# Moving the first two products of an FFN into the Mamba passes ahead of it

## The chip, the cores and the metric

The kernel runs on one core of one Trainium2 chip. The metric is the device time of one execution in microseconds, lower is better. The time before is 3401.91 us, the median of 3 runs (3400.91 to 3403.28).

## The reference, cut to what matters

The input x is (4, 2048, 256), float32. A Mamba layer is computed, then a feed-forward network (FFN) with ternary weights and a scale for each output column, each followed by a residual and a layer norm:

```python
xz = einsum('bld,ed->ble', x, in_proj_w); xs, z = xz[..., :512], xz[..., 512:]
u = silu(conv4(xs) + conv_b)                      # depthwise, 4 taps
dt_lo, B, C = split(einsum('bld,ed->ble', u, x_proj_w), (64, 16, 16))
delta = softplus(einsum('blr,dr->bld', dt_lo, dt_proj_w) + dt_proj_b)
h = exp(delta * A) * h + (delta * u) * B          # a scan over 2048 positions
y = (sum over n of h * C + u * D) * silu(z)
x1 = layernorm(x + einsum('bld,ed->ble', y, out_proj_w))
g = silu(x1 @ w1.T * s1) * (x1 @ w2.T * s2)       # w1, w2: 1024 x 256
g = gelu(g @ h1.T * sh1); g = gelu(g @ h2.T * sh2)    # h1, h2: 1024 x 1024
out = layernorm(x1 + g @ w3.T * s3)               # w3: 256 x 1024
```

## The kernel before, in words

The work is cut into 16 tiles of 512 positions (`NT`), four to a row of the batch. There are two stages, one after the other: all 16 tiles go through Mamba (`mamba_stage`), x1 is written to HBM, and then all 16 go through the FFN.

**The Mamba stage.** The scan has 64 groups of a tile (`NG`): each is one 128x512 scan on VectorE (`scan`, L759), whose decays ScalarE writes into one of three PSUM banks (`decay_of`, L563), two groups ahead (`EXP_LEAD`). Four groups make a chunk: before it VectorE (three chunks of four, L743) or GpSimd (the fourth, L645) makes the input `db`, behind it GpSimd multiplies with C (`times_c`, L634) and TensorE sums over n (`fold_step`, L412); behind every fourth chunk VectorE adds u*D (`skip`, L783). Each engine runs the same list by hand: `tile(t)` goes through slots i = 0 to 63, and in slot i it handles group i + 20 (`OFF`), so that from slot 44 on it scans the next tile. Beside the scan the slots hold everything else, one tile ahead: convolutions in slots 0 to 15 (L350, copies L485), silu of u in slot 17 (L494), the x_proj product in 18 to 21 (L364), z in 26 to 33 (L337, copies L482), silu of z in slot 40 (L490), spread rows (L391, copies L512) in 42 to 54, the products of the tile after (L325, copies L555) in 47 to 53, softplus in several (for the second quarter in slots 39 to 43: L521 to L536 on ScalarE, L766 and L770 on VectorE), the output product in 55 to 60 (L430). The layer norm of the tile before is in slots 1 to 11: statistics on VectorE, a few small steps on GpSimd in slot 8, and in slot 11 ScalarE writes x1 into `res` (L582). All queues are in order, and an instruction waits for semaphores; so a slot's place in a queue is also what it delays. All DMAs are issued by SyncE (SP): rows of delta to HBM (L248, L250), broadcasts back (L256, L265), inputs, x1.

**Between the stages** `round_weights` loads all FFN weights in 20 pieces of 128x1024 and 8 of 128x256, rounds them to float32r on ScalarE (L1236), and VectorE and TensorE check that the rounding lost nothing; the result is a flag (L1253), and all engines branch on it: with ternary weights the branch for exact weights (`split`) is taken.

**The FFN stage** (`ffn_stage`, split). Every activation is held as two float32r parts (high: a ScalarE copy, L1059; low: the difference, VectorE, L1123), so a product takes two matmuls. A tile on TensorE is: `hidden` layer 0, `hidden` layer 1 (128 matmuls of 512 columns each, L961, with the 8 transposes of the next x1, L973, in layer 1), `output` (64 matmuls of 256 columns, L1020), then `gated` of the next tile (64 matmuls of 512 columns on x1, L961 with `s_x_t`). ScalarE applies Silu in `gated` (L1066) and Gelu in `hidden` (L1082). The PSUM banks are two each for w1, w2, hidden and output.

In PSUM during the Mamba stage banks 0 and 1 are `p_mm`, 2 is `p_dt`, 3 `p_b`, 4 `p_y`, 5 to 7 the decays.

Of the kernel before, what the change touches and what calls it, by code (L numbers as in the profile page):

```python
# [5 lines left out]
F32 = mybir.dt.float32  # L6
# [77 lines left out]

OFF = 20
CONV_SLOTS = range(0, KI * TAPS)
SILU_U_SLOT = 17
# [16 lines left out]
EXP_LEAD = 2  # L104

# [25 lines left out]
def mamba_stage(nc, sems, xT, x, in_wT, conv_w, conv_b, xp_wT, dt_wT, dt_b, A_log, D_param, out_wT,  # L131
                fold, spread, ident, d_rows, du_rows, x1):
    ctx = ExitStack()
    with ctx:
# [23 lines left out]
        x_nat = sb("x_nat", [P, SUB, DM])  # L158
        res = sb("res", [P, SUB, DM])
        xb = sb("xb", [P, KI, TAPS - 1 + NT])  # L160
        uz = [sb(f"uz{i}", [P, 2 * KI, NT]) for i in range(2)]
# [16 lines left out]
        bc = [sb(f"bc{i}", [P, NT], F32R) for i in range(2)]  # L178

# [34 lines left out]
        DECAY0, SCANNED0, SAVED0, HC0, FOLDED0, DVE0, POOL0, OUT0 = 2 * GC, 2 * JC, NK, TURNS * QN, HCSTEPS, 2 * QV, 2, SUB + 1  # L214

        COPIES = 16 * GN

        block = ctx.enter_context(nc.Block())

        WEIGHTS = 12  # L220

        @block.sync
        def _(sp):
# [52 lines left out]
            load_xT(OPENING)  # L276
            copies(OPENING, 0)
# [30 lines left out]
        def _(pe):  # L308
# [21 lines left out]
            def z_product(t, j, k):  # L330
                if k == 0:
                    if j >= 2:
                        pe.wait_ge(z_sb, t.count(KI, j - 1))
                    elif j == 1:
                        pe.wait_ge(xd_sb, t.count(2, 2))
                        pe.wait_ge(xd_lo, t.count(1, 1))
                last = pe.matmul(p_mm[(1 + j) % 2][:], w_in[:, k, DI + j * P:DI + (j + 1) * P], xT_sb[:, k, :],  # L337
# [4 lines left out]
            def conv_product(t, j, k):  # L342
# [7 lines left out]
                last = pe.matmul(p_mm[j % 2][:], w_conv[:, j, k, :], xb[:, j, k:k + NT],  # L350
# [4 lines left out]
            def front(t, i):  # L355
                par = t.tt % 2
                if i in CONV_SLOTS:
                    conv_product(t, *divmod(i - CONV_SLOTS.start, TAPS))
                if i in XD_SLOTS:
# [4 lines left out]
                    last = pe.matmul(p_mm[0][0:DTR + 2 * NS, :], w_xp[:, k, :], uz[par][:, k, :],  # L364
# [8 lines left out]
            def step_sizes(t, c):  # L373
                pe.wait_ge(xd_sb, t.count(2, 2))
                if not (is_first(t) and c == 0):
                    pe.wait_ge(sp_dve, t.count(2 * KI, 2 * c))
                pe.matmul(p_dt[:], w_dt[:, c * P:(c + 1) * P], xd[:], start=True, stop=True).then_inc(dt_mm, 1)

            def rows(t, r):
                nxt = t.following()  # L380
                if r < 2:
                    pe.wait_ge(xd_lo, t.count(1, 1))
                    pe.wait_ge(z_sb, t.count(KI, 3 + r))
                else:
# [31 lines left out]
            def project(t, s, k_first, k_last):  # L416
                pe.wait_ge(gated, t.count(KI, k_last + 1))
# [942 lines left out]
```

## Time and profile before

| | |
|---|---|
| median of 3 runs | 3401.91 us |
| the profiled execution | 3402.25 us, its span 3400.4 us |
| Mamba stage | 0 to about 2021 us of the span |
| weights rounded and checked | about 2021 to 2058 us |
| FFN stage | about 2058 to 3400 us |
| DMA traffic | 223.8 MB in the queue of the kernel's own DMAs |

Busy shares of the whole span are averages over stages of different kinds; the slices of the span show them apart. The granted clock is TensorE's, 1.00 being full.

### The profile page before, as it was taken

To read this page: it belongs to the slowest core of one execution; us is meant where nothing else is said; L and a number is where in the kernel's file an instruction comes from. 1 tells how busy PE (TensorE), PEld (TensorE's weight loads), DVE (VectorE), ACT (ScalarE), POOL (GpSimd) and SP (SyncE) were. 2 spreads that over 40 slices of the span, in tenths; PEclk is the share of its full clock that TensorE was granted. 3 is DMA by queue.
4 is the path that set the end of the run, shared out by engine and by line. 5 is a ranking of instruction groups with operands and counts; after the bars stand their busy time and mean duration, and the time that the engine had idled before them with its cause. 6 is when DMAs were issued, how large, how long until landed. Compare 5 with 4: busy or idle time off the path is not lost. (4 is left out here: it accounts for less than half of the span.)

```text
span 3400.4 us, 37160 instructions
## 1 busy us (share of the span) xinstructions
PE 2667.5 (78%) x10431; PEld 1546.2 (45%) x10432; DVE 2371.5 (70%) x2860; ACT 1817.9 (53%) x2980; POOL 1738.6 (51%) x892
## 2 busy tenths in 40 slices
PE   5666776676676667667667438999999999999997
PEld 2121222122122212212222115888888888888886
DVE  2999999899999999999999964333343344344443
ACT  3667566666666666666675534444444444444442
POOL 1899998898898899898899950000000000000000
PEclk8777877788787788878778657999999999999999
DMA  3344433444433444433444321000000000000000
GB/s 85 85 99 112 107 97 89 106 106 100 111 91 91 106 112 106 97 98 91 99 112 105 96 99 68 13 13 13 13 13 13 12 13 12 13 12 13 12 13 13
DMA packets 138273, 225.80 MB, mean 66 GB/s; under 512 B 14432, under 2 KB 49120, under 8 KB 138080
## 3 DMA queue, kind: packets, MB, share of 16 engines
q1 hardware_dynamic: 138080, 223.80, 26.8%
q14 instruction: 142, 1.16, 0.1%
q8 instruction: 51, 0.84, 0.1%
HBM read 173.42 MB, written 50.33 MB: 66 GB/s over the span
## 5 line engine op out<-in xcount | busy, mean ns | idle before, releaser
L759 DVE TENSOR_TENSOR_SCAN h<-bank,state,db 128x512 f32<-128x512 f32 x1024 | 1250.4, 1263 | 54.9 <-ACT bank L563 28.4
L634 POOL TENSOR_TENSOR hc<-h,c_rows 128x1024 f32<-128x1024 f32 x512 | 1194.9, 2362 | 44.9 <-PE bank L412 34.3
L563 ACT ACTIVATE bank<-d_bc,a_neg 128x512 f32<-128x512 f32 x1024 | 699.2, 687 | 578.8 <-DVE h L759 577.0
L961 PE MATMUL s_bank<-s_act,weights_r 128*128 128x512 f32 x4096 | 935.0, 390 | 0.0
L961 PEld LDWEIGHTS s_bank<-s_act,weights_r 128*128 128x128 f32 x4096 | 768.1, 188 | 158.3
L1123 DVE TENSOR_TENSOR s_act<-s_h,s_act 128x512 fp32r<-128x512 f32 x384 | 262.7, 689 | 638.7 <-ACT s_act L1059 627.0
L391 PE MATMUL bank<-bc,w_spread 64*128 64x512 f32 x272 | 157.7, 604 | 420.9 <-DVE db L743 416.9
L1082 ACT ACTIVATE s_h<-s_bank,s_sc 128x512 f32<-128x512 f32 x256 | 176.0, 688 | 528.8 <-PE s_bank L961 528.6
L743 DVE TENSOR_TENSOR db<-bank,du_bc 128x2048 f32<-128x2048 f32 x192 | 434.7, 2264 | 21.2 <-DMA du_bc<-du_rows 21.1
L412 PE MATMUL bank<-hc,fold_w 128*32 128x512 f32 x2048 | 363.2, 790 | 95.2 <-DVE uz L783 78.7
L645 POOL TENSOR_TENSOR db<-du_bc,b_row 128x2048 f32<-128x2048 f32 x64 | 289.7, 4526 | 118.7 <-DVE h L759 106.2
L391 PEld LDWEIGHTS bank<-bc,w_spread 64*128 64x128 f32 x272 | 59.6, 233 | 632.4 <-DVE db L743 545.7
L350 PE MATMUL bank<-xb,w_conv 128*128 128x512 f32 x512 | 291.8, 700 | 6.5 <-issue 2.6
L1059 ACT ACTIVATE s_act<-s_h 128x512 fp32r<-128x512 f32 x384 | 241.7, 629 | 18.0 <-DVE s_h L1133 9.9
L961 PE MATMUL s_bank<-s_x_t,weights_r 128*128 128x512 f32 x1024 | 237.5, 393 | 1.4 <-DVE s_x_t L1117 1.4
L961 PEld LDWEIGHTS s_bank<-s_x_t,weights_r 128*128 128x128 f32 x1024 | 193.0, 190 | 41.3 <-DVE s_x_t L1117 1.8
L412 PEld LDWEIGHTS bank<-hc,fold_w 128*32 128x32 f32 x2048 | 45.2, 122 | 308.1 <-issue 202.1
L1066 ACT ACTIVATE s_silu<-s_bank,s_sc 128x512 f32<-128x512 f32 x128 | 88.3, 690 | 179.7 <-PE s_bank L961 171.8
L350 PEld LDWEIGHTS bank<-xb,w_conv 128*128 128x128 f32 x512 | 99.2, 214 | 171.9 <-issue 166.9
L364 PE MATMUL bank<-uz,w_xp 128*96 128x512 f32 x128 | 89.4, 814 | 97.4 <-ACT uz L494 97.4
L325 PE MATMUL bank<-xT_sb,w_in 128*128 128x512 f32 x256 | 144.3, 704 | 21.7 <-DVE a_neg L729 15.6
L1133 DVE SCALAR_TENSOR_TENSOR s_h<-s_bank,s_sc,s_silu 128x512 f32<-128x512 f32 x128 | 96.2, 751 | 82.6 <-PE s_bank L961 82.6
(91 smaller groups left out, 2299.0 us busy)
## 6 DMA issues: line engine op xcount, KB each, us to landing
d_bc<-d_rows SPq DMA_DIRECT2D x256, 256.0 KB, 4.7
du_bc<-du_rows SPq DMA_DIRECT2D x256, 256.0 KB, 7.6
d_rows<-sp_r SPq DMA_DIRECT2D x64, 256.0 KB, 2.0
du_rows<-sp_w SPq DMA_DIRECT2D x64, 256.0 KB, 2.0
xT_sb<-in_xT SPq DMA_DIRECT2D x16, 512.0 KB, 9.1
x_nat<-in_x SPq DMA_DIRECT2D x16, 512.0 KB, 4.6
x<-res SPq DMA_DIRECT2D x16, 512.0 KB, 3.2
s_x_nat<-x SPq DMA_DIRECT2D x16, 512.0 KB, 4.4
```

The lines of the kernel that those rows point to most:

```text
L350: last = pe.matmul(p_mm[j % 2][:], w_conv[:, j, k, :], xb[:, j, k:k + NT], start=k == 0, stop=k == TAPS - 1)
L391: pe.matmul(dst[:], spread_w[:, which, :], bc[t.tt % 2][DTR:P, :], start=True, stop=True).then_inc(done, 1)
L412: last = pe.matmul(p_y[GD * j:GD * j + GD, :], fold_w[:], hc[:, k % HCSTEPS, j, :], start=q == 0, stop=q == QN - 1, tile_position=(0, GD * j))
L563: act.activation(decays[DECAY_BANK[g]][:], d_bc[c % 2][:, j, :], ACT.Exp, scale=a_neg[:, g:g + 1]).then_inc(decay, 1)
L634: pool.tensor_tensor(hc[:, k % HCSTEPS, at:at + HG], h[:, H_SLOT[k], at:at + HG], c_rows[:, q, :].unsqueeze(1).broadcast_to([P, HG, NT]), ...
L645: pool.tensor_tensor(db[:, k % DBSTEPS], du_bc[c % 2][:], b_row[:].unsqueeze(1).broadcast_to([P, JC, NT]), ALU.mult).then_inc(db_pool, 1)
L743: dve.tensor_tensor(db[:, k % DBSTEPS], p_b[:].unsqueeze(1).broadcast_to([P, JC, NT]), du_bc[c % 2][:], ALU.mult).then_inc(db_dve, 1)
L759: dve.tensor_tensor_scan(h[:, H_SLOT[k], j, :], decays[DECAY_BANK[g]][:], db[:, k % DBSTEPS, j, :], state[:, g:g + 1], ALU.mult, ALU.add). ...
L961: last = pe.matmul(dst, weights[:, w_at + k * rows_w + cols:w_at + k * rows_w + cols + P], ins[j][:, k, :], start=k == 0 and j == 0, stop= ...
L1059: act.activation(acts[(c // KH) % 2][0][:, c % KH, :], hring[c % 3][:], ACT.Copy).then_inc(hi, 1)
L1082: act.activation(dst, p_h[m % 2][:], ACT.Gelu, scale=sc[:, 2 + layer, m:m + 1]).then_inc(gelu, 1)
L1123: dve.tensor_tensor(a[1][:, c % KH, :], hring[c % 3][:], a[0][:, c % KH, :].bitcast(F32), ALU.subtract).then_inc(lo, 1)
```

## The change

The products of x1 with w1 and w2 are made in the Mamba stage, one tile behind the norm, and go through HBM (`ab`, 16 x 256 KB for each tile). New in each `tile(t)` of the Mamba stage, where t is the tile whose residual is formed and x1 is that of the tile before it:

- TensorE: `ffn(t, i)` is called first in each slot. Slots 13 and 17: transposes of `res` (k = 0, 1; 4 blocks each, plain float32 matmuls against the identity). Slots 15 and 19: the same 4 blocks again and one float32r matmul that takes the high part off. Slots of `AB_PLACES`: 16 products of 4 float32r matmuls of 512 columns, into banks 0 to 2.
- ScalarE: last in slots 14, 16, 18, 20 a copy of `x_t`; last in the slot after each product a copy of it to one of three buffers; first in the slot after that its store, a DMA that ScalarE issues; behind every second copy a load of 256 KB of w1 and w2.
- SP: the load of x goes straight into `res` (the buffer `x_nat` is gone), behind `copies(t, 3)`, and waits for the store of x1 and the transposes.
- u of quarter 0 is in one buffer `u0` for both tiles: the convolutions run in the order 1, 2, 3, 0, and the Silu of u is two instructions.
- At the start w1 and w2 (2 MB) are loaded into buffers of h, rounded on ScalarE in slots 2 and 8 of the pass before the first tile, and stored to HBM in pieces of 256 KB; VectorE waits for the roundings before its first tile. After the last tile the transposes and 16 products of the last x1 run by themselves (`PAST`).
- `round_weights` still checks all 28 pieces, but keeps only h1, h2, w3.

In the FFN stage (`split_stage`) `transposes` and the products of `gated` are gone. SP loads pairs of products into a ring of four; ScalarE applies Silu to four at a time in SBUF (slot m = 1 of each layer), then one high copy at m = 2 to 5; VectorE follows with product and low part. `hidden` has four PSUM banks in place of two.

```diff
+CONV_ORDER = (1, 2, 3, 0)
+XT_PLACES = ((13, 2), (17, 1))
+AB_PLACES = ((25, 0), (30, 2), (32, 2), (34, 2), (35, 1), (36, 2), (38, 1), (40, 1), (41, 0), (44, 2), (46, 2),
+             (48, 2), (50, 2), (52, 2), (60, 2), (62, 2))
+ABRING = 3
...
 # SP, tile(t)
-                sp.wait_ge(out_sb, t.count(SUB, OUT0))
+                copies(t, 3)
+                sp.wait_ge(x1_out, t.count(16, 16))
+                sp.wait_ge(xt_mm, t.count(KM, KM))
-                sp.dma_start(x_nat[:], x[t.b, rows, :].rearrange("(s p) c -> p s c", p=P)).then_inc(x_in, 16)
-                copies(t, 3)
+                sp.dma_start(res[:], x[t.b, rows, :].rearrange("(s p) c -> p s c", p=P)).then_inc(x_in, 16)
...
 # TensorE
+            def transpose(dst, k, alone):
+                for s in range(SUB):
+                    last = pe.matmul(dst[:, s * P:(s + 1) * P], res[:, s, k * P:(k + 1) * P], w_id[:].bitcast(F32),
+                                     start=s == 0, stop=alone and s == SUB - 1)
+                return last
+            def transposed(t, k, step):
+                dst = bank[XT_PLACES[k][1]]
+                if step == 0:
+                    if k == 0:
+                        pe.wait_ge(ln_out, t.count(SUB, SUB))
...
+                    elif exists(t.following()):
+                        pe.wait_ge(conv_sb, t.following().count(KI, KI))
+                    transpose(dst, k, True).then_inc(tr_mm, 1)
+                elif step == 2:
+                    pe.wait_ge(xt_hi, t.count(KM, k + 1))
+                    transpose(dst, k, False)
+                    pe.matmul(dst[:], w_id[:], x_t[0][:, k, :], start=False, stop=True).then_inc(xt_mm, 1)
+            def ffn_product(t, e):
+                m, which = divmod(e, 2)
...
+                for k in range(KM):
+                    for j in range(2):
+                        last = pe.matmul(product_bank(t, e)[:], w12_sb[m % 2][:, which, k, :], x_t[j][:, k, :],
+                                         start=k == 0 and j == 0, stop=k == KM - 1 and j == 1)
+                last.then_inc(ab_mm, 1)
...
                 for i in range(NG):
                     n = OFF + i
+                    if exists(t):
+                        ffn(t, i)
                     if n % JC == 1:
...
+            for i in range(NG):
+                ffn(PAST, i)
 # ScalarE
+            def load_w12(t, m):
+                act.dma_start(w12_sb[m % 2][:].bitcast(F32), w12[m]).then_inc(w12_in[m % 2], 16)
+            def store(t, e):
+                act.wait_ge(ab_sb, ab_done(t, e + 1))
+                act.dma_start(at, ab_sbuf[e % ABRING][:]).then_inc(ab_out[e % ABRING], 16)
+            def ffn(t, i):
+                for k in range(KM):
+                    src = bank[XT_PLACES[k][1]]
+                    if i == XT_PLACES[k][0] + 1:
+                        act.wait_ge(tr_mm, t.count(KM, k + 1))
+                        act.activation(x_t[0][:, k, :], src[:], ACT.Copy, scale=-1.0).then_inc(xt_hi, 1)
+                    elif i == XT_PLACES[k][0] + 3:
+                        act.wait_ge(xt_mm, t.count(KM, k + 1))
+                        act.activation(x_t[1][:, k, :], src[:], ACT.Copy, scale=-1.0).then_inc(xt_lo, 1)
+                for e in range(AB):
+                    if i == AB_PLACES[e][0] + 1:
+                        act.wait_ge(ab_mm, t.count(AB, e + 1))
+                        act.wait_ge(ab_out[e % ABRING], t.count(ab_uses(e), 16 * (e // ABRING) + ABOUT0))
+                        act.activation(ab_sbuf[e % ABRING][:], product_bank(t, e)[:], ACT.Copy,
+                                       scale=-1.0).then_inc(ab_sb, 1)
+                        m = e // 2 + 2
+                        if e % 2 == 1 and m < KH:
+                            load_w12(t, m)
+                        elif e % 2 == 1 and exists(t):
+                            load_w12(t.following(), m - KH)
...
 # ScalarE in the FFN stage, at m of layer 0 and 1: gated(next tile, layer, m - 1)
+            def gated(t, half, step):
+                if step == 0:
+                    for m in range(RING):
+                        gate_silu(t, half * RING + m)
+                elif step <= RING:
+                    gate_high(t, half * RING + step - 1)
```

## Rows read from the trace of the kernel before

**Rows 1.** The page: engine busy times, and the span in 40 slices.
```profile
PE 2667.5 (78%) x10431; PEld 1546.2 (45%) x10432; DVE 2371.5 (70%) x2860; ACT 1817.9 (53%) x2980; POOL 1738.6 (51%) x892
...
PE   5666776676676667667667438999999999999997
```

**Rows 2.** Busy times of one steady Mamba tile (span; PE, PEld, DVE, ACT, POOL, clock, DMA).
```profile
1510.14:1630.50 120.36, 81.48 (x257) 27.09 (x257) 113.26 (x102) 77.76 (x133) 108.97 (x57) 0.81 0.43 103
1510.00:1524.00 14.00, 4.82 (x13) 1.48 (x13) 12.74 (x10) 10.68 (x16) 14.00 (x8) 0.50 0.08 27
```

**Rows 3.** Waits of VectorE from 100 to 1990 us: total, times, longest.
```profile
DVE uz L783 <- PE bank L412: 35.1, 15, 2.4
DVE h L759 <- ACT bank L563: 28.4, 16, 2.1
DVE h L759 <- POOL hc L634: 25.9, 16, 1.7
DVE bank L766 <- ACT bank L536: 13.9, 15, 1.0
```

**Rows 4.** Waits of ScalarE in the tile of rows 2.
```profile
ACT bank L563 <- DVE h L759: 34.5, 33, 2.9
ACT res L582 <- POOL nb L686: 5.3, 1, 5.3
```

**Rows 5.** The chain that ended last, first FFN tile (start us, us, what).
```profile
2062.18 3.95 DMA s_x_nat<-x
...
2069.61 60.60 PE s_bank L961 x256
2130.21 0.87 PE s_bank L973 x8
2131.09 14.54 PE s_bank L961 x64
```

**Rows 6.** Timeline between the stages and in the first FFN tile (start us, us, engine).
```profile
2057.82 0.14 DVE L1253 TENSOR_SCALAR flag<-losses 1x1 int32<-1x1 f32 x1
...
2086.53 38.70 PE L961 MATMUL s_bank<-s_act,weights_r 128*128 128x512 f32 x170
```

**Rows 7.** Groups of instructions of the kinds added: busy us, mean ns.
```profile
L430 PE MATMUL bank<-w_out,uz 128*128 128x256 f32 x512 | 129.6, 403 | 19.8 <-POOL uz L663 19.5 <-DVE res L790 0.3
L482 ACT ACTIVATE uz<-bank 128x512 f32<-128x512 f32 x64 | 37.4, 584 | 20.9 <-PE bank L337 20.9
```

**Rows 8.** DMA issue of 128x512 float32 by SP: ns min/median/max.
```profile
L248 SPq DMA_DIRECT2D d_rows<-sp_r x64: 330/338/495, 59.4 to 1946.4; - x64
```

**Rows 9.** Timeline of slots 11 to 19 of a steady Mamba tile.
```profile
1580.56 2.08 ACT L582 ACTIVATE res<-res,nb,y 128x256 f32<-128x256 f32 x4 [5.25 <-POOL nb L686]
1580.79 1.99 PE L350 MATMUL bank<-xb,w_conv 128*128 128x512 f32 x4
...
1582.70 1.07 PE L412 MATMUL bank<-hc,fold_w 128*32 128x512 f32 x8
...
1587.77 1.28 ACT L494 ACT_TABLE_LOAD   x1
...
1591.12 1.99 PE L364 MATMUL bank<-uz,w_xp 128*96 128x512 f32 x2 [6.29 <-ACT uz L494]
...
1595.05 0.75 DVE L783 SCALAR_TENSOR_TENSOR uz<-uz,dpar,bank 128x512 f32<-128x512 f32 x1 [2.43 <-PE bank L412]
```

**Rows 10.** Timeline of slots 34 to 42 of the tile before it.
```profile
1501.05 0.69 ACT L563 ACTIVATE bank<-d_bc,a_neg 128x512 f32<-128x512 f32 x1 [2.56 <-DVE h L759]
...
1517.09 0.70 DVE L766 SCALAR_TENSOR_TENSOR bank<-sp_w,bank 128x512 f32<-128x512 f32 x1 [0.96 <-ACT bank L536]
```

**Rows 11.** Waits of ScalarE from 1501 to 1517.1 us.
```profile
ACT bank L563 <- DVE h L759: 5.0, 5, 2.6
```

**Rows 12.** Timeline of the end of the Mamba stage.
```profile
2015.75 2.07 ACT L582 ACTIVATE res<-res,nb,y 128x256 f32<-128x256 f32 x4 [2.62 <-POOL nb L686]
...
2021.29 0.83 SPq L1230 DMA_DIRECT2D stage<-in_w1T  x2
```

More of the change, by code:

```diff
@@ L276, in _ @@
             load_xT(OPENING)
+            for piece, src in enumerate(w[k * P:(k + 1) * P, :] for w in (w1T, w2T) for k in range(KM)):
+                sp.dma_start(w12_piece(piece), src).then_inc(w12_raw, 16)
             copies(OPENING, 0)
@@ L475, in _ @@
             act.sem_inc(decay, DECAY0)
+            act.sem_inc(xt_lo, XT0)
+            act.sem_inc(ab_sb, AB0)
+            for k in range(ABRING):
+                act.sem_inc(ab_out[k], ABOUT0)
             def front(t, i):
@@ L585, in _, with ffn_stores @@
+            def ffn_stores(t, i):
+                for e in range(AB):
+                    if i == AB_PLACES[e][0] + 2:
+                        store(t, e)
             for i in range(X_SLOTS[0], X_SLOTS[-1] + 2):
@@ L879, in sem @@
     def sem(name):
[L880 removed]
+        return sems.enter_context(nc.semaphore("s_" + name))
+    RING, HBANKS = 4, 4
     x_nat = [sb(f"x_nat{i}", [P, SUB, DM]) for i in range(2)]
[L883 to L885 removed]
+    ends = [[sb(f"end{i}{j}", [P, KH, NT], F32R) for j in range(parts)] for i in range(2)]
@@ new lines, in split_stage @@
+    p_h, p_o = bank[0:HBANKS], bank[HBANKS:]
+    consts_in, stored = sem("consts_in"), sem("stored")
+    x_in = [sem("x_in0"), sem("x_in1")]
+    ab_in = [sem(f"ab_in{i}") for i in range(RING)]
+    h_mm, o_mm = sem("h_mm"), sem("o_mm")
+    silu, gate, gate_hi, gate_lo = sem("silu"), sem("gate"), sem("gate_hi"), sem("gate_lo")
+    gelu, hi, lo = sem("gelu"), sem("hi"), sem("lo")
+    scaled, summed = sem("scaled"), sem("summed")
+    ln_dve, ln_out = sem("ln_dve"), sem("ln_out")
+    waited = sem("waited")
@@ L886, in ffn_stage, with float32_stage, sb, sem @@
+def float32_stage(nc, sems, ctx, branch, weights, x1, scales, s3, ident, out):
+    def sb(name, shape, dt=F32):
+        return ctx.enter_context(nc.sbuf_tensor("g_" + name, shape, dt))
+    def sem(name):
+        return sems.enter_context(nc.semaphore("g_" + name))
+    x_nat = [sb(f"x_nat{i}", [P, SUB, DM]) for i in range(2)]
+    x_t = [sb(f"x_t{i}", [P, KM, NT]) for i in range(2)]
+    acts = [sb(f"act{i}", [P, KH, NT]) for i in range(2)]
     silu_t = [sb(f"silu{i}", [P, NT]) for i in range(2)]
@@ L959, in product @@
                         wait(k)
-                    for j in range(parts):
-                        last = pe.matmul(dst, weights[:, w_at + k * rows_w + cols:w_at + k * rows_w + cols + P],
-                                         ins[j][:, k, :], start=k == 0 and j == 0,
-                                         stop=k == n_k - 1 and j == parts - 1)
+                    last = pe.matmul(dst, weights[:, w_at + k * rows_w + cols:w_at + k * rows_w + cols + P],
+                                     ins[:, k, :], start=k == 0, stop=k == n_k - 1)
                 return last
@@ L1235, in _ @@
                     act.wait_ge(loaded[i % ring], 16 * (i // ring + 1))
-                    act.activation(weights[:, at[i]:at[i] + cols[i]], stage[i % ring][:, 0:cols[i]],
-                                   ACT.Copy).then_inc(rounded, 1)
+                    if 2 <= i and at[i] < ROUNDED_FROM:
+                        act.wait_ge(took, i - 1)
+                    act.activation(place(i), stage[i % ring][:, 0:cols[i]], ACT.Copy).then_inc(rounded, 1)
             @block.vector
```

480 lines of the change are left out of this document (372 added, 108 removed).

## Prediction

> **What bounds the kernel now.** I read the page first for the stages: TensorE is busy in tenths of 5 to 7 up to about 2021 us of the span and at 9 from 2058 us on [rows 1]. So there are two kernels with two bounds. In the FFN stage the chain of waits is TensorE's own matmuls, one behind the other [rows 5]: what leaves its queue leaves the time. In the Mamba stage a tile takes 120.36 us, of which VectorE works 113.26, GpSimd 108.97, TensorE 81.48 and ScalarE 77.76 [rows 2]. VectorE is the bound, with 7 us of waits: for TensorE in `skip` (35.1 us in all), for ScalarE's decays (28.4), for GpSimd (25.9) and for ScalarE in softplus (13.9), 103 us over 15 tiles [rows 3]. ScalarE waits 34.5 us of a tile for VectorE's scans and 5.3 for GpSimd's norm [rows 4]: there is room, but it is spread, and the decays are only two groups ahead. The question is what the moved work does at the few slots without room.
>
> **What the FFN stage gives back.** A tile loses 64 matmuls of 512 columns and 8 transposes. In the chain 64 such matmuls take 14.54 us and the transposes 0.87 [rows 5]: 15.41 us, for 15 tiles 231.2 us. ScalarE's new groups of four don't put it back: for a tile it has 16 Gelu, 8 Silu and 24 copies at about 0.65 us and 4 table loads of 1.28 [rows 9], 36 us beside 66 us of TensorE, and behind m = 1 it has four banks, or 3 x 3.6 us, to catch up 5 us. The first tile starts with loads instead: before, the flag was set at 2057.96 [rows 6], the load was out at 2062.18 and had landed after 3.95 us [rows 5], and layer 0 began at 2086.53 [rows 6], so that its first product ended at 2090.2. Now eight 512 KB pieces have to pass ScalarE (8 Silu, 8 copies, one table: 12 us) and VectorE; with a first piece at 2066 and a wait for a ring of four, the last low part is there at about 2082.5 and the product ends at 2082.8: 7.4 us saved, with 0 (the loads are slow) and 12 as bounds. Together 238.6 us.
>
> **What the Mamba stage pays, by place.** Prices: a copy out of PSUM 0.58 us [rows 7], 0.62 with its gap; a store of 128x512 float32 costs SP 0.34 us of its queue [rows 8], and ScalarE must first see the copy ended, so copy and store are 1.0 us of ScalarE; a product is 4 matmuls, 0.91 us by rows 5 and 1.8 at the low clock. A tile adds to ScalarE 20 copies and 16 stores, 18.5 us, and 8 loads whose issue (0.34) lies beside a running copy. That is less than the 34.5 us of rows 4; no trace shows an issue on ScalarE, so 0 to 0.5 us is its range.
> The Trainium skill (DMA: Bandwidth & Descriptors, Issuing engines are not separate DMA queues) says that the time to initiate a DMA is usually small beside the transfer; by that alone the stores would be free, some 0.4 us a piece less, while rows 8 put it in an in-order queue.
> - Slots 11 to 19, the dearest. x1 is complete at 1582.64 (L582, its start and 2.08 [rows 9]). TensorE had the convolutions of slots 13 and 14 out from 1580.79 on. Now at the head of slot 13 it waits for x1, so behind 1582.64 come 8 transposing instructions of 128 columns. The nearest are 256 columns at 0.25 us (129.6/512 [rows 7]); I take 0.2, bounds 0.13 and 0.35, so 1.6 us. Then a spread row (0.5), 4 convolution instructions (0.43 each, from 4 in 1.99 with their tail), the fold (1.07), the 8 again with the float32r matmul (1.8), the last convolution (1.1): it ends at about 1590.5. ScalarE copies it and `x_t` and makes a decay (2.0), so the table load of Silu starts at 1592.5, before at 1587.77: 4.7 us late. Behind it are TensorE's x_proj product, the fold of slot 18 and VectorE's `skip`, which already waited 2.43 us [rows 9]: no slack. TensorE's shorter idle stretch may keep the clock up, which would make product and fold (1.99 for two instructions, and twice 1.07, at the low clock) 1 to 2 us shorter. I take 4.0, bounds 1.9 and 7.
> - Slots 19 to 33. The second transposes sit between the x_proj products; their result is some 0.6 us later than before beside VectorE, which subtracts from it in slot 23. I take 0.6, bounds 0 and 2.
> - Slots 34 to 42. ScalarE is there the tightest: from 1501.05 on [rows 10] it waits 5.0 less the 2.56 ahead of that, 2.4 us in 16 [rows 10, 11], and L766 at 1517.09 already waited 0.96 for its Ln [rows 10]. Added ahead of it are copies in slots 35, 36, 37 and 39 and stores in 34, 36, 37, 38 and 40, 4 x 0.62 and 5 x 0.4: 4.5, less 2.4. I take 2.2, bounds 0.5 and 5 (TensorE at the low clock, as it was here, 0.50 [rows 2], delivers late).
> - Slots 46 to 58. Five more products stand ahead of five rows and x products, and the next softplus ends some 2 us later by my estimate, and VectorE didn't wait for this one. I take 0.9, bounds 0 and 3.
> Sum 7.7 us for a tile (2.4 to 17). It counts for the 15 tiles that have a next one: 115.5 us. Below nothing is excluded, as no work is taken from VectorE.
> SP's new waits cost nothing: x1's store and the transposes are done by slot 20, and what is queued behind them, `copies` of the next tile, isn't due before slot 31; `copies(t, 3)` is no longer behind the load of x. GpSimd's gate of quarter 0 is 11 slots ahead of the copy that now waits for it. The 4 MB of stores a tile are 33 GB/s beside 103 at a DMA share of 0.43 [rows 2]: hidden by the margin of the broadcasts, up to 1 us a tile without it.
>
> **Start and end.** At the start the rounding of w1 and w2 waits for its own stores in slot 8 while two convolutions are due: I take 2 us, 0 to 8. At the end x1 was complete at 2017.8 and the next loads were out at 2021.29 [rows 12]. Now behind 2017.8 come 4 rounds of transposes at the low clock (2 us each) with 3 copies, 10 us, then 16 products that ScalarE paces with copy, store and weight load (1.2 to 1.3 us each, 20 us), and the last store lands 2 to 3 us later, less the 3 us that x1's store took: 30 us, 22 to 40.
>
> **Sum.** Against the profiled execution, 3402.25 us (span 3400.4, and 1.85 around it; the median is 0.34 less): 3402.2 - 238.6 + 115.5 + 2 + 30 = 3311.
>
> **The rivals.**
> Freed queues (faster): ScalarE's 34.5 us of waits [rows 4] take everything and the fuller TensorE holds its clock from slot 13 on, so that fold and x_proj product win back what the transposes cost. For it: the clock was 0.81 in the mean and 0.50 in the emptiest stretch [rows 2]. Against: the 5.3 us for which x1 is waited for stay. Then a tile pays 2.5 us: 3402.2 - 238.6 + 37.5 + 28 = 3229.
> The Trainium skill (TensorE: Matmul & The Clock Gate, Why this matters for your kernels) states that idle gaps between bursts bring the low clock back and sustained work the full one; by that rule the products would be partly paid by the clock, which is this case.
> Slower than before: TensorE's queue becomes the bound. Where the added work runs at 1.2 GHz, it is 64 matmuls at 0.45 and 34 at 0.35 us, 41 us, on 81.48 of 120.36 [rows 2]: 122 us of work in an in-order queue that also waits for x1 in slot 13 and for copies in 30 to 52. A tile then takes some 136 us, 16 more: 3402.2 - 238.6 + 240 + 40 = 3444. It decides from (238.6 - 32)/15 = 13.8 us a tile on. Against it: the new work fills gaps such as the 6.29 us ahead of 1591.12 [rows 9].
> Stores against broadcasts: the transfers for `du_bc` come later and L743 waits for them; 1 to 2 us a tile more, 3326 to 3341. It stays inside the range.
> That the change does nothing of what it says can be excluded for the FFN stage, where the matmuls are simply fewer.
>
> **How the numbers follow.** The forecast 0.60 (it lies between 3265 and 3385 by its bounds), freed queues 0.22, the queue as the bound 0.10, and 0.08 for the forecast with contention. The range reaches to the freed queues and most of the dearer outcomes: 3228 to 3390. Faster by over 0.2% (7 us, about what a measurement of this kernel can tell) needs under 13.4 us a tile: 0.88. Within 0.2%: 0.03. Slower: 0.09.
>
> **What would show it.** In the FFN stage tiles 66.5 us apart instead of 81.9 and its first product ended near 2083 us plus the shift; between x1 and the next loads 33 us instead of 3.5. In the Mamba stage a tile of 128 us: `skip` of slot 19 waiting 6 us for the fold, L766 of slot 42 waiting 3 us for Ln, and TensorE waiting for L582 in slot 13. I'd be wrong if the tile stays at 122 (then the waits were covered) or passes 134, if ScalarE shows waits for the products of L961's kind, or if VectorE waits for `du_bc`.

## The result and the profile after

The changed kernel takes 3435.22 us (median of 4 runs, 3429.69 to 3443.06), the kernel before 3401.41 us on the same chip (3400.07 to 3403.28): ratio 1.0101, 95% interval 1.0079 to 1.0122. It is 1% slower, a small difference but clear of the noise. The forecast was 3311 us with a range of 3228 to 3390, and 0.09 for slower: it was wrong.

The profiled execution took 3429.69 us, the lowest of the four. Its page (engine busy times, then the span in 40 slices) shows where the boundary between the stages now lies:
```profile
span 3427.8 us, 40081 instructions
...
PE 2793.9 (82%) x10946; PEld 1626.3 (47%) x10946; DVE 2349.3 (69%) x2829; ACT 2021.8 (59%) x3344; POOL 1747.4 (51%) x892
...
PE   5787787777777877777778687567999999999997
```
Against rows 1 the nines of the FFN stage begin three slices later, and there are 11 instead of 14. Four marks divide the two spans. The start of the last four L719 pieces (L582 before [rows 12]) is 2243.26 against 2015.75; the first load of the next stage and the last store of products are in the timeline of the end (start us, us, engine):
```profile
2243.26 2.07 ACT L719 ACTIVATE res<-res,nb,y 128x256 f32<-128x256 f32 x4 [2.62 <-POOL nb L890]
...
2279.51 0.34 ACTq L744 DMA_DIRECT2D ab<-ab  x1
2281.97 0.83 SPq L1664 DMA_DIRECT2D stage<-in_w1T  x2
```
and the first output product of the FFN began at 2403.9 (L1204), before at 2145.4 (L1020), from the first and last starts of these lines:
```profile
L1204 PE MATMUL s_bank<-weights_r,s_end x1024: 277/283/386, 2403.9 to 3409.5; 128*128 128x256 f32 x171
```
```profile
L1020 PE MATMUL s_bank<-weights_r,s_act x1024: 277/283/387, 2145.4 to 3382.1; 128*128 128x256 f32 x171
```
So the 27.4 us by which the span grew are: Mamba stage up to x1 complete +227.5; from there to the first load of the FFN weights 36.6 us in place of 3.5, +33.2; rounding and first FFN tile -2.2; the rest of the FFN 1023.9 us in place of 1255.0, -231.1. An FFN tile is now 66.5 us, in the chain of waits (start us, us); the first line is a load ahead of the first tile:
```profile
2324.34 7.02 DMA s_abr<-ab
...
2406.27 6.26 PE s_bank L1204 x50
2412.53 58.07 PE s_bank L1191 x256
2472.01 0.70 DVE s_end L1306
2472.75 6.26 PE s_bank L1204 x50
```
Everything but the first term is about as forecast. The Mamba tile is the question: the Silu of z runs from 62.7 us in the first to 2095.5 in the last of 16 tiles, 135.5 us apart, before 120.3. It gained 15.2 us; 7.7 were forecast. One steady tile by engine (columns as in rows 2):
```profile
1558.60:1695.20 136.60, 105.72 (x355) 44.43 (x355) 113.76 (x101) 87.55 (x154) 109.11 (x55) 0.85 0.48 135
```
VectorE's work is what it was (113.26), so the whole gain is waits. Those of VectorE over some 14 tiles (170 to 2000 us: total, times, longest), and below them the last row from the kernel before, over the stretch of rows 3:
```profile
DVE uz L988 <- PE bank L482: 84.5, 18, 6.2
DVE bank L971 <- ACT bank L673: 78.1, 14, 5.7
DVE h L964 <- ACT bank L700: 52.8, 34, 3.3
DVE db L948 <- DMA du_bc<-du_rows: 48.4, 23, 4.7
DVE h L964 <- POOL hc L839: 22.7, 14, 1.8
DVE bc L982 <- ACT bc L636: 7.5, 13, 0.9
...
DVE db L743 <- DMA du_bc<-du_rows: 5.6, 4, 2.3
```
Against rows 3, per tile: `skip` behind the fold 6.0 in place of 2.3; softplus (L971) 5.6 in place of 0.9; decays 3.8 in place of 1.9; and 3.5 for `du_bc`, a wait that was 5.6 us in all over 15 tiles before. The second and the fourth were not forecast at this size. By their places in the timeline, some 20 of the 52.8 us for decays come around the Silu of z (slots 38 to 44), where there were none before; nearly all the rest stands behind the norm and behind the copy of the last convolution. Of the 48.4 us for `du_bc` half come shortly before the Silu of z (about slot 38), half 30 to 40 us behind it (about slot 56).

**What happens in slots 34 to 42.** The Ln is the last ScalarE step of the softplus, L673, and the dt product (L446) is what the softplus starts from. The timeline of one tile (start us, us, engine, idle before it and what ended it):
```profile
1536.35 2.90 SPq L321 DMA_DIRECT2D du_bc<-du_rows  x4
...
1537.29 0.35 ACTq L738 DMA_DIRECT2D w<-w  x1
...
1546.02 2.07 PE L547 MATMUL bank<-x_t,w 128*128 128x512 f32 x4 [5.76 <-DMA w<-w]
...
1548.02 2.07 PE L446 MATMUL bank<-xd,w_dt 64*128 64x512 f32 x2
...
1550.13 0.69 ACT L658 ACTIVATE sp_e<-bank,dtb 128x512 f32<-128x512 f32 x1 [6.07 <-PE bank L446]
...
1553.29 1.28 ACT L626 ACT_TABLE_LOAD   x1
...
1557.80 0.69 ACT L666 ACTIVATE sp_r<-bank,dtb 128x512 f32<-128x512 f32 x1
...
1560.24 0.70 DVE L971 SCALAR_TENSOR_TENSOR bank<-sp_w,bank 128x512 f32<-128x512 f32 x1 [5.57 <-ACT bank L673]
```
Read it from below, as far as this one tile shows. VectorE waits for ScalarE's Ln; ahead of it stood 4.5 us of Silu of z with two table loads; ScalarE began the softplus late, because TensorE's dt product was late; and that stood in the queue behind the product of slot 38, which waited 5.8 us for its weights. The load had been issued at 1537.29 and landed about 8.7 us later. Why so late is in the DMA view of 1534 to 1547 us (busy tenths of the 16 DMA engines in 40 slices, then issues with the median us to landing):
```profile
DMA  9982969979999999999999999999999999999999
...
ab<-ab ACTq DMA_DIRECT2D x4, 256.0 KB, 8.4
du_bc<-du_rows SPq DMA_DIRECT2D x4, 256.0 KB, 8.7
w<-w ACTq DMA_DIRECT2D x2, 256.0 KB, 8.6
```
The DMA engines are at nine tenths and more nearly all the time. Beside the eight broadcasts and four stores, the 512 KB load of the next x for the projections (`xT_sb`, 11.0 us to landing) falls into the same stretch. The engines were as busy in the kernel before, in the same slots (1495 to 1508 us, the same view), for the last 8 us of it:
```profile
DMA  0010298008910949999999999999999999999999
...
du_bc<-du_rows SPq DMA_DIRECT2D x4, 256.0 KB, 7.6
```
Over the whole kernel a weight load lands after 2.5, 3.5 or 9.7 us (least, median, most). The Trainium skill (DMA: Bandwidth & Descriptors, Issuing engines are not separate DMA queues) says that DMAs of any issuing engine run on the same 16 DMA engines and interleave; the rows agree.

**Slots 11 to 19** went much as the prediction has them: the norm's result, the transposes that waited for it, the last convolution's copy, x_proj behind the Silu of u, and the skip behind the fold:
```profile
1489.73 2.08 ACT L719 ACTIVATE res<-res,nb,y 128x256 f32<-128x256 f32 x4 [5.19 <-POOL nb L890]
...
1491.93 1.15 PE L506 MATMUL bank<-w_id,res 128*128 128x128 f32 x8 [2.83 <-ACT res L719]
...
1500.28 0.69 ACT L621 ACTIVATE u<-bank,cb 128x512 f32<-128x512 f32 x1 [4.30 <-PE bank L415]
...
1505.52 2.02 PE L428 MATMUL bank<-u,w_xp 128*96 128x512 f32 x2 [3.35 <-ACT u L631]
...
1509.48 0.75 DVE L988 SCALAR_TENSOR_TENSOR uz<-uz,dpar,bank 128x512 f32<-128x512 f32 x1 [6.13 <-PE bank L482]
```

### The profile page after: what moved, and what is told of

It is laid out like the page before. It is cut to its first block and busy times, and to the rows that moved or that the text cites. A ratio compares the mean times of both kernels' runs of the same rounds, so it can differ in the third digit from the quotient of the medians.

```text
span 3427.8 us, 40081 instructions
## 1 busy us (share of the span) xinstructions
PE 2793.9 (82%) x10946; PEld 1626.3 (47%) x10946; DVE 2349.3 (69%) x2829; ACT 2021.8 (59%) x3344; POOL 1747.4 (51%) x892
## 5 line engine op out<-in xcount | busy, mean ns | idle before, releaser
L964 DVE TENSOR_TENSOR_SCAN h<-bank,state,db 128x512 f32<-128x512 f32 x1024 | 1254.5, 1265 | 87.9 <-ACT bank L700 60.2
L1191 PE MATMUL s_bank<-s_end,weights_r 128*128 128x512 f32 x2048 | 472.1, 392 | 22.5 <-DVE s_end L1284 22.4
L547 PE MATMUL bank<-x_t,w 128*128 128x512 f32 x1088 | 379.8, 483 | 114.2 <-DMA w<-w 88.0
L1191 PE MATMUL s_bank<-s_mid,weights_r 128*128 128x512 f32 x2048 | 466.8, 389 | 0.0
L1191 PEld LDWEIGHTS s_bank<-s_end,weights_r 128*128 128x128 f32 x2048 | 385.5, 189 | 104.4 <-DVE s_end L1284 25.0
L1191 PEld LDWEIGHTS s_bank<-s_mid,weights_r 128*128 128x128 f32 x2048 | 384.4, 188 | 79.8
L547 PEld LDWEIGHTS bank<-x_t,w 128*128 128x128 f32 x1088 | 224.3, 220 | 305.5 <-issue 131.6
L482 PE MATMUL bank<-hc,fold_w 128*32 128x512 f32 x2048 | 344.5, 752 | 18.8 <-DVE u L988 15.8
L1306 DVE TENSOR_TENSOR s_end<-s_h,s_end 128x512 fp32r<-128x512 f32 x128 | 88.5, 692 | 279.5 <-ACT s_end L1254 279.5
L1306 DVE TENSOR_TENSOR s_mid<-s_h,s_mid 128x512 fp32r<-128x512 f32 x128 | 87.1, 690 | 192.0 <-ACT s_mid L1254 192.0
L760 ACT ACTIVATE ab<-bank 128x512 f32<-128x512 f32 x272 | 158.9, 584 | 31.4 <-PE bank L547 30.9
```

What stands on the lines that cost most here:

```text
L482: last = pe.matmul(p_y[GD * j:GD * j + GD, :], fold_w[:], hc[:, k % HCSTEPS, j, :], start=q == 0, stop=q == QN - 1, tile_position=(0, GD * j))
L547: last = pe.matmul(product_bank(t, e)[:], w12_sb[m % 2][:, which, k, :], x_t[j][:, k, :], start=k == 0 and j == 0, stop=k == KM - 1 and j ...
L964: dve.tensor_tensor_scan(h[:, H_SLOT[k], j, :], decays[DECAY_BANK[g]][:], db[:, k % DBSTEPS, j, :], state[:, g:g + 1], ALU.mult, ALU.add). ...
L1191: last = pe.matmul(p_h[m % HBANKS][:], weights[:, at:at + P], ins[j][:, k, :], start=k == 0 and j == 0, stop=k == KH - 1 and j == parts - 1)
L1306: dve.tensor_tensor(dst[1][:, m, :], hring[c % RING][:], dst[0][:, m, :].bitcast(F32), ALU.subtract).then_inc(lo, 1)
```

## The experiments

Theory A: loads that land behind the broadcasts hold up TensorE's in-order queue. Its rival B: ScalarE's own added work is what is late. Theory B of experiments 6 and 8: the transposes ahead of the fold make the skip late. C: the stores crowd out the broadcasts. D: what remains is the order in ScalarE's queue. Each run is timed beside the kernel before on the same chip, whose median was 3402 to 3403 us. "First" and "last" mean the place of the call `ffn(t, i)` in each of TensorE's slots. A tile's time is, as above, the distance of the Silus of z.

**1. What is left without the products** (e11_noprod).
```diff
-                        ffn_product(t, e)
+                        if exists(t):
+                            pe.sem_inc(ab_mm, 1)
+                        else:
+                            ffn_product(t, e)
...
+                        if exists(t):
+                            act.sem_inc(ab_sb, 1)
+                            if e % 2 == 1:
+                                act.sem_inc(w12_in[(e // 2) % 2], 16)
+                            continue
                         act.wait_ge(ab_mm, t.count(AB, e + 1))
```


> Edit, on the changed kernel: in the 16 tiles of the Mamba stage the products, their copies and stores and the weight loads are left out, replaced by semaphore increments; transposes, x_t copies, the loads of x into res and the order of the convolutions stay, and the products of the last x1 are made, with the weights of pairs 0 and 1, and read by every tile of the FFN stage (left out: all other products of w1 and w2). It prices what is left: by the prediction's terms for slots 11 to 19 and 19 to 33 that is 4 to 5 us a tile over the 120.3 of before, so 3435 - 15 x 10.5 = 3278, range 3260 to 3295. If the products and their traffic cost all of it: 3200 to 3215. If the transposes cost more than measured: over 3300.


Measured: 3282.43 us (3272.8 to 3285.55), a tile 126.5 us. So transposes, the new load of x and the order of the convolutions cost 6.2 us a tile, products and their traffic 9.0. VectorE's waits over 14 tiles say where (170 to 1990 us; its lines stand 3 to 11 lower than in the changed kernel, so L999 is the skip, L982 the softplus):
```profile
DVE uz L999 <- PE bank L482: 86.0, 14, 6.2
DVE h L975 <- ACT bank L703: 44.1, 28, 1.8
...
DVE bank L982 <- ACT bank L676: 14.2, 15, 1.0
```
The wait of `skip` is all there without a single product, that of softplus is what it was before the change: the one belongs to what this run keeps (transposes, load of x and order of the convolutions, which it doesn't tell apart), the other to the products.

**2. Is it TensorE's work?** (e10_quarter)
```diff
-                for k in range(KM):
-                    for j in range(2):
-                        last = pe.matmul(product_bank(t, e)[:], w12_sb[m % 2][:, which, k, :], x_t[j][:, k, :],
-                                         start=k == 0 and j == 0, stop=k == KM - 1 and j == 1)
+                last = pe.matmul(product_bank(t, e)[:], w12_sb[m % 2][:, which, 0, :], x_t[0][:, 0, :],
+                                 start=True, stop=True)
```


> Edit, on the changed kernel: each of the 16 products of a tile is one matmul (k = 0, high part) instead of four; copies, stores, loads and all waits stay (left out: three quarters of each product with w1 and w2). It takes 48 matmuls, 19 to 25 us of TensorE's 105.7, out of a tile. Theory A (the loads' landing and the order, not TensorE's work, cost the time): a tile takes 132 to 135, 3385 to 3430. Rival 2 of the prediction (TensorE's queue has become the bound): 5 us a tile or more, under 3360.


Measured: 3414.8 us (3408.99 to 3418.4), a tile 134.7. Taking 48 of 64 matmuls out gives 0.8 us a tile and 20 us in all. The theory's range for the time holds it. TensorE's busy time in a tile fell less than the 19 to 25 us expected, from 105.7 to 95.4, and the granted clock fell with it, from 0.85 to 0.80 (columns as in rows 2):
```profile
1558.00:1692.71 134.71, 95.40 (x302) 36.03 (x306) 111.59 (x100) 85.49 (x152) 108.17 (x55) 0.80 0.49 134
```
Even so 10.3 us less work gave 0.8 us, and TensorE's wait for the weights grew from 79.1 to 95.2 us: its amount of work isn't the bound.

**3. The weight loads** (e1_held).
```diff
-                            load_w12(t, m)
+                            act.sem_inc(w12_in[m % 2], 16)
...
-                            load_w12(t.following(), m - KH)
+                            act.sem_inc(w12_in[m % 2], 16)
```


> Edit: the weights of pairs 0 and 1 are loaded once and held; the other 120-odd loads of 256 KB are replaced by a semaphore increment on ScalarE at the same place (left out: the products of pairs 2 to 7 use the weights of pairs 0 and 1). Theory A (of the 15.2 us that a Mamba tile has gained, the largest part, the 4.65 of the wait of L971 and 1.9 of the decays, is a load that lands late, behind the broadcasts, with the dt product of slot 38 behind the waiting product in TensorE's queue): the wait of 5.8 us at slot 38 goes, L971 waits under 1.5 us, a tile takes 127 to 130 us, 3330 to 3370 us in all. Rival B (ScalarE's own added copies and stores, or TensorE at its low clock, are what the softplus waits for): a tile stays at 134 or more, 3415 to 3435. If loads also delay the broadcasts, the 3.2 us a tile of waits for du_bc shrink as well (below 1.5) and the time is 3310 to 3340.


Measured: 3361.1 us (3352.77 to 3368.19), ratio 0.9872, a tile 131.2. The time is as theory A had it, but not the row that I had named:
```profile
DVE bank L971 <- ACT bank L673: 64.1, 14, 5.5
...
DVE db L948 <- DMA du_bc<-du_rows: 3.3, 7, 0.7
```
L971 still waits 4.6 us a tile, where under 1.5 were expected; what went is the wait for `du_bc`. So the late load explains about 1 us of the softplus's wait. ScalarE's wait for the dt product is gone (0.7 us in all, before 84.2) and L971 waits on. TensorE's waits name the next obstacle: the dt product, no longer behind a waiting product, waits for a copy of the product in its own bank (28.2 us), and such a copy waits in turn for the store three before it (24.3 us).

**4. The order in TensorE's slots** (e2_last).
```diff
-                    if exists(t):
-                        ffn(t, i)
                     if n % JC == 1:
...
                             fold_step(now, g // JC)
+                    if exists(t):
+                        ffn(t, i)
```


> Edit: ffn(t, i) is called last in each of TensorE's slots instead of first; nothing else. Theory A: the dt product of slot 38 and the fold of slot 38 run ahead of the product that waits for its weights; L971 waits 1 to 2 us in place of 5.6, the waits of ScalarE for L446 fall from 90 us to under 30; 4 to 6 us a tile, 3345 to 3380. The skip of slot 19 gains at most 1 us. Rival (the product's wait only passes on: the next spread row and fold stand behind it in the queue in any order): 3420 to 3440, with the waits for spread rows grown. Rival B (ScalarE is what is late): no change, 3425 to 3440.


Measured: 3362.09 us (3358.52 to 3363.34), ratio 0.9876 [0.9859, 0.9892], a tile 130.7: 73 us from where one call stands. With nothing else changed it is 1.2% faster than the kernel before. Half of the row fell as expected and half not:
```profile
DVE bank L971 <- ACT bank L673: 68.4, 14, 5.6
DVE uz L988 <- PE bank L482: 63.2, 27, 5.6
DVE db L948 <- DMA du_bc<-du_rows: 34.8, 23, 3.3
DVE h L964 <- ACT bank L700: 30.3, 25, 1.8
```
ScalarE's wait for L446 is 3.7 us instead of 84.2 and TensorE's for the weights 2.2 instead of 79.1, but L971 waits on; `skip`, the decays and `du_bc` gave the time instead. These are other rows than in experiment 3, so that both runs took some 73 us is no proof that they took the same 73; no run has both edits.

**5. The stores** (e5_nostore).
```diff
+                if exists(t):
+                    act.sem_inc(ab_out[e % ABRING], 16)
+                else:
                     act.dma_start(at, ab_sbuf[e % ABRING][:]).then_inc(ab_out[e % ABRING], 16)
...
-                src = ab[1:TILES + 1].rearrange("(b q) e p t -> b q e p t", q=2)[t.b, t.tt, 2 * m:2 * m + 2]
+                src = ab[TILES, 2 * m:2 * m + 2]
```


> Edit, on the changed kernel: ScalarE's 16 stores of a tile (256 KB each) are replaced by a semaphore increment at the same place; only the products of the last x1 are stored, and every tile of the FFN stage loads those, the same 4 MB (left out: the products of 15 of the 16 tiles never reach the FFN stage). Theory C (the 3.2 us a tile of VectorE's waits for du_bc come of the 4 MB of stores beside the broadcasts): they fall under 0.8 us a tile, ScalarE has 5.4 us a tile less to issue, and the weight loads land sooner: 3340 to 3390. Rival (the loads of w1 and w2 are what collides with the broadcasts; holding them took the waits from 48.4 to 3.3 us already): the waits for du_bc stay above 1.5 us a tile, 3400 to 3435.


Measured: 3432.47 us (3420.03 to 3436.39), a tile 135.7. Taking 4 MB a tile out changes nothing; the wait for `du_bc` is 37.7 us, for the weight loads 92.4. Theory C falls, and so does the idea that the stores' issues on ScalarE cost. The same edit with no product stored at all (e4_nostore) has no time.

**6. The transposes later** (e3_xt): `XT_PLACES = ((19, 2), (19, 1))`.


> Edit: the transposes for k = 0 and 1 go from slots 13 and 17 to slot 19, those of the second step from slots 15 and 19 to 21, their copies on ScalarE to slots 20 and 22. Theory (the skip of slot 19 waits 3.7 us a tile more because transposes that wait for the norm, 2.8 us, and run at the low clock stand ahead of the convolutions and the fold of slot 18): L988 behind the fold waits about 2.5 us a tile in place of 6, a tile takes 131 to 132.5, 3375 to 3395. Rival (the low clock of TensorE in slots 11 to 19 and the late silu of u set the fold, not the queue): the wait of L988 stays above 5 us, 3425 to 3440. Against it stands that the x_proj products and the dt product of slot 24 come behind the moved transposes: up to +2 us a tile back, 3410.


Measured: 3421.38 us (3406.63 to 3429.09), a tile 134.6. The expected 3375 to 3395 missed. `skip` waits less, 3.5 us a tile where 2.5 were expected, so the transposes' place in the queue is part of its wait; but the low rows take over (170 to 2000 us):
```profile
DVE uz L988 <- PE bank L482: 49.6, 22, 3.5
DVE bc L982 <- ACT bc L636: 44.8, 13, 4.2
```

**7. ScalarE's queue** (e6_behind, e7_siluz), on top of e2_last. The first calls `ffn_stores(t, i)` behind `decay_of(now, g)` instead of ahead of it; the second has `SILU_Z_SLOT = 42` besides.


> Edit, on top of e2_last: in ScalarE's slots the store comes behind the decay instead of ahead of it. A store waits until the copy before it has landed (0.62 us, 102 to 120 times in the row of decays that wait for ab), and with the decay between them that wait is covered. Theory D (what remains in slots 34 to 42 once TensorE's order is mended is ScalarE: 8 copies, 8 stores and 4 loads beside softplus and the Silu of z, with no gap between 1500.87 and 1508.5 in e2_last): some 4.5 us of ScalarE's time a tile come free, half of it on the path; 3325 to 3345, the wait of L971 falls from 4.9 to 3 to 4 us a tile. Rival (ScalarE's order hides it; what L971 waits for is the dt product, which waits for its bank): 3352 to 3362 as e2_last.


Measured: 3355.72 us (3353.08 to 3363.58), ratio 0.9867 [0.9851, 0.9884], which can't be told from e2_last. The expectation (3325 to 3345) failed: the row of 0.62 us waits behind copies, 65.9 us in e2_last, is gone and the time stayed, so they lay in ScalarE's slack.


> Edit, on top of e6_behind: the Silu of z goes from slot 40 to slot 42 (SILU_Z_SLOT), behind the last step of the second quarter's softplus instead of ahead of its second step. It and its two table loads take 4.5 us (1501.58 to 1506.09 in e2_last), and the Relu, the Ln and then VectorE's L971 stand behind it. Theory D: L971 waits under 1.5 us a tile, 3 us a tile less than e6_behind, 3285 to 3310. Rival (the decays and the row copies of slots 42 to 44 pay for it instead): L971's wait goes, those of the scans for L700 grow by as much, and the time stays within 10 us of e6_behind.


Measured: 3334.05 us (3332.21 to 3337.61), a tile 128.8. The expected 3285 to 3310 missed. L971 waits 16.0 us in 14 tiles instead of 57.5, as expected, and `du_bc` 27.8 instead of 46.2; but 16 us come back as waits for decays (34.2 to 50.3) and 17 as `skip` (64.0 to 81.5). It is the first of these edits but e11_noprod's that takes the wait of the softplus away.

**8. The fold behind x_proj** (e8_xt, e9_xd), on top of e7_siluz. In e8_xt `XT_PLACES = ((16, 2), (20, 1))`, in e9_xd `XD_SLOTS = range(19, 19 + KI)`.


> Edit, on top of e7_siluz: the transposes go to slots 16 and 20 (from 13 and 17), their second step to 18 and 22. Theory B (transposes ahead of the fold of slot 18 delay the skip of slot 19): L988 behind the fold waits 2 us a tile in place of 4.2, 15 to 35 us less than e7_siluz. Rival (as in e3_xt, they now stand ahead of the x_proj products and the rows; the low rows waited 3.2 us a tile there): the wait of L982 grows by 2 us and the time stays within 10 us of e7_siluz.


Measured: 3331.61 us (3325.47 to 3338.5), a tile 128.9: no difference, where 15 to 35 us were expected; `skip` and the low rows together wait 85.1 us instead of 93.3, and the decays 60.2 instead of 50.3.


> Edit, on top of e7_siluz: the x_proj products go one slot later, to 19 to 22 (XD_SLOTS). In e7_siluz the one of slot 18 waits 3.8 us a tile for the Silu of u, with the fold of slot 18 behind it, and VectorE's skip of slot 19 waits 5.8 us a tile in all behind folds. Theory B2 (what the skip waits for is the late Silu of u, through the x_proj product in front of the fold; the transposes only make the Silu late): the wait of L988 falls to 2 to 3 us a tile, the low rows wait 1 us more, 3285 to 3310. Rival (as in e8_xt, the wait only moves to the low rows and the decays): 3325 to 3335.


Measured: 3314.27 us (3310.86 to 3316.43), a tile 127.4. The wait of `skip` falls to 29.4 us in 14 tiles, 2.1 each, the low rows' to 0.9 in all. The time is just outside the expected 3285 to 3310. With the filler called last, what `skip` waited for was the late Silu of u, by way of the x_proj product that stood ahead of the fold of slot 18. The decays now wait 116.9 us, so part of it moved.

**9. The bank of the dt product** (e12_bank0), on top of e9_xd.
```diff
-AB_PLACES = ((25, 0), (30, 2), (32, 2), (34, 2), (35, 1), (36, 2), (38, 1), (40, 1), (41, 0), (44, 2), (46, 2),
+AB_PLACES = ((25, 0), (30, 2), (32, 2), (34, 2), (35, 1), (36, 0), (38, 1), (40, 1), (41, 0), (44, 2), (46, 2),
...
-                    pe.wait_ge(ab_sb, ab_done(tile_before(t), (6, 14, 16)[c - 1]))
+                    pe.wait_ge(ab_sb, ab_done(tile_before(t), (4, 14, 16)[c - 1]))
...
-                    elif e in (4, 8):
+                    elif e in (4, 5, 8):
```


> Edit, on top of e9_xd: the product of slot 36 goes to PSUM bank 0 instead of bank 2, which is p_dt, so the dt product of slot 38 waits for 4 copies of the tile instead of 6. In e9_xd it waits 68.9 us in 15 times for such a copy, and in one tile that copy waited 4.3 us for the store three before it, with the decays of two scans behind it (VectorE waited 3.1 us for the first). If the copy of slot 37 is on the path through the dt product: L446's wait goes, ScalarE's Abs comes earlier, 15 to 30 us less, 3285 to 3300. Rival (the full ring of three copy buffers holds up ScalarE itself, in whatever bank the product lies): the waits of L760 for a store (50.6 us) and of the scans for L700 stay, 3308 to 3318.


Measured: 3281.13 us (3279.94 to 3288.28), ratio 0.9652 [0.9636, 0.9668], a tile 125.5. That is 3.5% faster than the kernel before and 4.5% faster than the changed one, and 33 us under e9_xd: somewhat better than expected: the wait of the dt product for its bank was on the path. The rival's row stays as well, though: L760 waits 56.7 us for stores. TensorE's waits in it (170 to 1960 us):
```profile
PE bank L547 <- DMA w<-w: 79.9, 16, 6.9
...
PE bank L446 <- ACT bc L636: 5.3, 14, 0.5
```
The weights land as late as ever, up to 6.9 us, and it costs little: the dt product no longer stands behind them, and ScalarE's wait for it is not among its waits any more. What is left of VectorE's waits is mostly for decays:
```profile
DVE h L964 <- ACT bank L700: 108.0, 77, 4.2
DVE uz L988 <- PE bank L482: 28.7, 14, 3.0
```

**10. Does the order still matter?** (e13_first): e9_xd with `ffn(t, i)` first again.


> Edit: e9_xd with ffn(t, i) first in TensorE's slots again, so the changed kernel with the store behind the decay, the Silu of z in slot 42 and x_proj from slot 19. It tells whether the order in the slot still matters once ScalarE's and the x_proj's places are mended. Theory A (a product that waits for a late load holds up the dt product and the fold behind it): 40 us or more above e9_xd, 3355 to 3385, with waits of ScalarE for L446 above 50 us. Rival (the order mattered only through the queues that the other edits have relieved): 3310 to 3330.


Measured: 3390.8 us (3387.66 to 3393.94), a tile 133.1: 76.5 us over e9_xd, more than the expected 3355 to 3385. ScalarE waits 64.8 us for L446, and TensorE 79.0 us for the weights, which was 0.3 in e9_xd. The order in TensorE's slots is worth the same 73 to 77 us with the other edits as without them.

## Why the prediction was wrong

- **FFN stage**: right. -231.2 forecast, -231.1 measured; 66.5 us a tile. First tile: 7.4 forecast, 2.2 measured. The term was mis-sized: a 512 KB piece that the chain passes took 7 us to land, and I had let all eight through in 16 us. The 2.2 lies inside its bounds of 0 and 12.
- **Between the stages**: 30 us forecast, 33.2 measured: right.
- **Start**: 2 us forecast; the Silu of z of the first tile stands at 62.7 instead of 64.8, so nothing was lost there.
- **Slots 11 to 19**: 4.0 us forecast, 3.7 measured on `skip`, and by e11_noprod it is there without any product. The size and the place are right; that the Silu of u and the x_proj product are on that path was named, and e9_xd shows it. **Slots 19 to 33**: 0.6 forecast, 0.5 measured on the low rows. All that e11_noprod has is 6.2 us a tile, some 4.7 of it on `skip` and the low rows; the rest is mostly decays (44.1 us in 14 tiles, 1.3 more a tile than before): a scan waits 1.4 us for the decay that stands in ScalarE's queue behind the copy of the last convolution, which no term had. The expectation for that kernel was 3278 us and it took 3282, which is partly luck: its tile cost 6.2 where 4 to 5 were expected, and from x1 complete to the first load it took 29.4 us instead of 36.6, which the expectation had left out.
- **Slots 34 to 42**: the step that failed. "Added ahead of it are copies ... and stores ...: 4.5, less 2.4. I take 2.2, bounds 0.5 and 5": it counts ScalarE's busy time and leaves out what each instruction waits for. Of the 8 loads it says that their "issue (0.34) lies beside a running copy"; when they land appears nowhere, nor that a product waits for it in an in-order queue ahead of the dt product. On L971 4.7 us a tile more were measured, on the decays of these slots some 1.5, and half of the new wait for `du_bc`, 1.7, lies here too: 7.9 together, above its upper bound. How far the queue of TensorE explains it, the rows tell: order (e2_last, e13_first) and loads (e1_held) are worth 73 to 77 us each, but the softplus's own wait of 5.6 us only goes to 4.9 and 4.6 by them, and from 4.1 to 1.1 when the Silu of z is put behind it (e6_behind, e7_siluz). So ScalarE's queue, the term's own mechanism, was part of it and was mis-sized; TensorE's order and the load's landing it left out.
- **Slots 46 to 58**: 0.9 forecast, for a softplus that VectorE never waits for; the other half of the wait for `du_bc`, 1.7 us a tile, lies here.
- **The stores and the broadcasts**: "33 GB/s beside 103 at a DMA share of 0.43 [rows 2]: hidden by the margin". The mean over a tile was the wrong number. From 1500 to 1508 us, from slot 34 on, the DMA engines were at nine tenths before the change; a transfer put in there landed after 8 to 9 us. The stores didn't matter, as forecast; the loads, a transfer with a reader waiting, did: 3.2 us a tile on `du_bc`, which e1_held takes away. The rival "stores against broadcasts" had this row, the wait for `du_bc`, at 1 to 2 us a tile, but not its cause: without the stores 37.7 of its 48.4 us stay.
- **The range**: the terms' own bounds go up to 17 us a tile, which is 3402.2 - 238.6 + 255 + 2 + 30 = 3451, and the 15.2 measured lies inside them; the range stopped at 3390. Of the signs of being wrong two came: a tile above 134 and waits for `du_bc`. Waits of ScalarE for products did not (0.4 us).
- **The rival** "TensorE's queue becomes the bound" gave 3444 us and 16 more a tile, close to the 3435 and 15.2 that came, but by its sum of work, which was wrong, so the closeness is luck. Its queue is what e2_last and e13_first show; its work is not: e10_quarter takes three quarters of the products' matmuls away for 20 us in all, and in the tile shown TensorE is busy 105.7 of 136.6 us, not 122. It got 0.10 because I weighed it as a sum of busy times. Freed queues: no row of VectorE's waits shows a gain of more than 0.1 us a tile, and the tile is 15 us longer, although the mean clock rose from 0.81 to 0.85.

What stays open: whether the time that the order costs and the time that the loads cost are the same, as no run holds the loads with the filler last. And why holding the loads takes the waits for `du_bc` from 48.4 to 3.3 us while taking the stores, twice the bytes, leaves 37.7. Loads and broadcasts both read HBM and write SBUF, stores the other way; no run here separates that from the places at which each is issued. The moves in ScalarE's queue (stores behind the decay, Silu of z in slot 42) were not made on the changed kernel by themselves: e13_first has them together with the later x_proj and is 44 us faster than it. A version with all of w1 and w2 kept in SBUF, or with a fourth copy buffer, wasn't tried.

## What to carry to other kernels

When filler work is moved into an in-order queue, put it behind what the bound engine waits for, in each slot: here its waits, more than its work, are what it passed on. Cost a new transfer by when it lands, read from the DMA engines' load in those very microseconds and not from the mean of a tile, and look at who stands behind its reader. And where one wait is removed and the time stays, follow the same instruction back one more step: here dt product, PSUM bank, Silu of z and x_proj were found one behind the other, and a few moves of places and calls turned 1% slower into 3.5% faster.

## What the hardware showed that I had not expected

A 256 KB load landed after 2.5 us at the least and after 8.6 us among eight 256 KB broadcasts, four stores and a 512 KB load; beside it even SP's issue of four broadcasts stretched from 1.74 to 2.90 us. 4 MB of stores a tile, of some 18 MB that it moves (135 GB/s over 136.6 us), cost no time that could be measured. With three quarters of the products' matmuls gone the granted clock of a tile was 0.80 instead of 0.85, and of the products' 22.4 us of busy time a tile 9.8 stayed. After the 5.8 us in which TensorE waited for its weights the granted clock from 1546 to 1552 us was 0.50, the lower level of 1.2 GHz, and both the product and the dt product took 2.07 us, which take 1.20 and 1.12 at the higher level, so a late transfer is paid for again by what follows it:
```profile
1546.00:1552.00 6.00, 5.93 (x14) 1.86 (x14) 4.05 (x3) 1.80 (x3) 2.79 (x2) 0.50 0.58 221
```
